# Turning attention weights: TensorE transposes against VectorE 32x32 blocks and quadrant DMAs

## The chip, the core and the metric

The kernel is one program on one core of a Trainium2 chip. The metric is the device time of one execution in microseconds (us), the median of several runs. The engines are TensorE (PE in the profile; PEld is its weight load), VectorE (DVE), ScalarE (ACT), GpSimd (POOL) and SyncE (SP), which here only issues DMAs.

## The reference, cut to what matters

Four graph layers follow each other on x of 32 batches x 256 nodes x 128 features; after each one the input is added and the rows are normalised. All is float32. The third layer (attention) and the fourth (two graph convolutions and four LSTM sweeps) are where the change lies:

```
# layer 3: attention over the 256 nodes
Wh = h @ W;  s1 = Wh @ a1;  s2 = Wh @ a2
e = s1[:, :, None] + s2[:, None, :];  e = where(e >= 0, e, 0.2 * e)
e = where(adj == 0, -inf, e);  h' = softmax(e, axis=-1) @ Wh
# layer 4
h = relu(adj @ (x @ Wg0 + bg0));  h = relu(adj @ (h @ Wg1 + bg1))
for p in 1..4:  h[p-1::p] = last hidden state of an LSTM over windows of p nodes
```

## The kernel before

The 32 batches are worked in 8 groups of 4 (GB = 4). The first two layers need sums over all batches and come first; groups 0 and 1 of layer 3 are worked on their own; then a loop of slots (`slots`, s = 2 to 10) runs three things side by side, written out by hand in each engine's program: attention of group s (A, s = 2 to 7), graph convolution of group s - 1 (B), LSTM of group s - 2 (L), and the last normalisation of group s - 3 (T). Each engine works its own list strictly in order, and semaphores tie the lists together.

The LSTM has eleven steps a group, k = 0 to 10. For step k TensorE works `x(k)` (line 855: input part) and `h(k)` (line 867: recurrent part, which needs the hidden state of step k - 1), ScalarE the gates' tanh (line 1231), VectorE `inner(k)` (lines 1712, 1718, 1722), ScalarE the cell's tanh (line 1267), and VectorE `state(k)` (line 1740), which releases `h(k + 1)`.

Attention of a group: ScalarE writes the exponentials of batch b into E1 (`a_exps`, line 1194, two instructions of 256 columns and their accumulator reads); E1 has the target node on the partitions and the source node along the columns. The mixing matmul (`a_mix`, line 791: two matmuls of 256 columns a batch, two records each) contracts over source nodes, so E1 must be turned. Before, TensorE does that: `a_turn_e` (line 770) works 16 transposes of 128x128 a group into PSUM, after `x(8)` and ahead of `h(8)`, and VectorE copies them into MS (`a_weights`, line 1640, four copies of 512 columns). Then come `h(8)`, `x(9)`, `a_mix` for batches 0 to 2, `a_project_mix` (line 801) for 0 and 1, `h(9)`, `x(10)`, `a_mix` for batch 3, and the rest. `a_hidden` (line 1700) is the relu of the second graph convolution on VectorE: it reads all of PSUM tensor PA, into which line 838 has written, and its result is read by `x(0)` of the next slot.

SP's list holds the loads at the start, and then one output DMA a group (line 425), which waits for GpSimd's last normalisation.

MS and E1 are planes 0 and 1 of `late`, a part of the on-chip tensor HB; a plane has 2048 columns, and COLS is 1024, so a half plane (h = 0 or 1) holds two batches.

Of the kernel before, what the change touches and what calls it, by code (L numbers as in the profile page):

```python
# [27 lines left out]
GB = 4  # L28
# [72 lines left out]
def build(nc, x, xt, adj, early_in, later_in, lstm_w, out):  # L101
    ctx = ExitStack()
    with ctx:
# [18 lines left out]
        MS, E1 = (late[:, k, :].rearrange("p (t n) -> p t n", n=NODES) for k in range(2))  # L122
        HS = late[:, 3, 0:2 * BANK].rearrange("p (k n) -> p k n", k=2)
        ZF = late[:, 3, 2 * BANK:4 * BANK]

        AN = late[:, 0, 0:BANK].rearrange("p (c n) -> p c n", c=NC)
        DIAG = late[:, 2, 0:NC * P].rearrange("p (c n) -> p c n", c=NC)
# [105 lines left out]
        def before(g):  # L233
# [15 lines left out]
        agg0_ps, loop_ok, first_ok, second_ok, both_ok, mix1, mix3, norm_ok, diag_ok, turned_ok = (  # L249
            sem(n) for n in ("agg0_ps", "loop_ok", "first_ok", "second_ok", "both_ok", "mix1", "mix3", "norm_ok", "diag_ok",  # L250
                             "turned_ok"))
        copied_ok = sem("copied_ok")
        f_half, cf_half, cell_half, tc_half = (sem(n) for n in ("f_half", "cf_half", "cell_half", "tc_half"))
        lane1 = [sem(f"{n}_lane1") for n in ("g_ps", "g_ok", "ca_ok", "cf_ok", "cell_ok", "tc_ok", "h_ok")]
        rows_ok, dots_ok, s12_ok, px_ps, px_ok = (sem(n) for n in ("rows_ok", "dots_ok", "s12_ok", "px_ps", "px_ok"))
# [140 lines left out]
        @block.sync  # L396
        def _(sp):
            def load_xt(g):
                sp.dma_start(XT[:, g % NX], xt[g]).then_inc(xt_in[g % NX], 16)

            def load_x(g):
                sp.dma_start(XIN[:, g % NX], x[g]).then_inc(x_in[g % NX], 16)

            sp.dma_start(AD[:, 1], adj[:, 1]).then_inc(adjt_in, 16)
            load_x(0)
            sp.dma_start(early[:], early_in).then_inc(early_ok, 16)
            load_xt(0)
            sp.dma_start(AD[:, 0], adj[:, 0]).then_inc(adj_in, 16)
            load_x(1)
            load_xt(1)  # L410
            load_x(2)
            load_xt(2)
            sp.dma_start(later[:], later_in).then_inc(later_ok, 16)
            load_xt(3)
            load_x(3)
            for g in range(NX, GROUPS):
                sp.wait_ge(gate_ps, g - NX + 1) if g - NX < DIRECT else sp.wait_ge(gate_x, g - NX + 1 - DIRECT)
                load_xt(g)
                sp.wait_ge(mix3, g - NX + 1)
                load_x(g)  # L420
            sp.dma_start(WT[:], lstm_w).then_inc(lstm_in, 16)

            for g in range(GROUPS - 1):
                sp.wait_ge(ln[3]["out"], TILES * (g + 1))
                sp.dma_start(out[g], OUT[:, g % 2]).then_inc(sent[g % 2], 16)
            half = TILES // 2 * P
            sp.wait_ge(last_act, TILES // 2)
            sp.dma_start(out[GROUPS - 1][:, 0:half], OUT[:, 1, 0:half]).then_inc(sent[1], 16)
            sp.wait_ge(last_dve, LAST_DVE)
            sp.wait_ge(last_act, TILES - LAST_DVE)  # L430
            sp.dma_start(out[GROUPS - 1][:, half:], OUT[:, 1, half:]).then_inc(sent[1], 16)
            sp.wait_ge(sent[0], 16 * (GROUPS // 2))
            sp.wait_ge(sent[1], 16 * (GROUPS // 2 + 1))
# [129 lines left out]
        def _(pe):  # L563
# [221 lines left out]
            def a_mix(g, some):  # L785
                pe.wait_ge(ln[1]["out"], TILES * (g + 1))
                f = front(g)
                for b in some:
                    pe.wait_ge(pt_ok, GB * (g - 1) + b + 1)
                    for m in range(NC):  # L790
                        mm = pe.matmul(f.AB[b][:, 0:NODES], turned(X2, m, b), f.MS[:, 2 * b + m, :],  # L791
                                       start=(m == 0), stop=(m == NC - 1))
                    mm.then_inc(px_ps, 1)

# [124 lines left out]
            def slot(s, par, A, B, L, T):  # L919
                def x(k):  # L920
                    lstm_x(s - 2, par, k) if L else None

                def h(k):
                    lstm_h(s - 2, k) if L else None

                if s == LAST + 2:
                    lstm_x(LAST, par, 0)
                    t_turn(s - 3, 1 - par)
                    lstm_x(LAST, par, 1)
                    for k in range(LANED, NSTEP):  # L930
                        for l in range(2):

                            if STEPS[k][1] == 0:
                                lane_x(par, k, l)
                                lane_x(par, k + 1, l) if k > LANED and l == 0 else None
                            else:
                                lane_x(par, k, l) if STEPS[k][1] > 1 or l == 1 or k == LANED + 1 else None
                                lane_h(k, l)
                    t_turn_half(par, 0)
                    spin(Q[F][:, 0:P], 8)  # L940
                    t_turn_half(par, 1)
                    return
                if not L and not A and not B:
                    return

                if s == LAST + 1:
                    x(0)
                    x(1)
                    t_turn(s - 3, 1 - par)
                    a_spread0(LAST, (0, 1), 0)  # L950
                    x(2)
                    x(3)
                    h(3)
                    a_spread0(LAST, (2, 3), 1)
                    a_weigh0(LAST, 0)
                    spin(PB[:, BANK:BANK + P], 4)
                    x(4)
                    a_weigh0(LAST, 1)
                    x(5)
                    h(5)  # L960
                    x(6)
                    a_weigh1(LAST)
                    h(6)
                    a_spread1(LAST)
                    for k in range(7, NSTEP):
                        x(k)
                        h(k) if STEPS[k][1] else None
                    return
                x(0)
                a_residual(s) if A else None  # L970
                x(1)
                t_turn(s - 3, 1 - par) if T else None
                a_spread0(s - 1, (0, 1)) if B else None
                x(2)
                a_spread0(s - 1, (2, 3)) if B else None
                x(3)
                h(3)
                a_rows(s) if A else None
                a_weigh0(s - 1) if B else None
                x(4)  # L980
                x(5)
                h(5)
                x(6)
                a_weigh1(s - 1) if B else None
                h(6)
                a_spread1(s - 1) if B else None
                x(7)
                x(8)
                a_turn_e(s, range(GB)) if A else None
                h(8)  # L990
                x(9)
                if A:
                    a_mix(s, (0, 1, 2))
                    a_project_mix(s, (0, 1))
                h(9)
                x(10)
                if A:
                    a_mix(s, (3,))
                    a_project_mix(s, (2,))
                h(10)  # L1000
                a_project_mix(s, (3,)) if A else None
# [57 lines left out]
        def _(act):  # L1059
# [115 lines left out]
            def a_lin(g, some):  # L1175
                f = front(g)
                for b in some:
                    act.wait_ge(wh_ok, 2 * g + b // 2 + 1) if g < 2 else act.wait_ge(s12_ok, g - 1)
                    act.wait_ge(max_ok, TILES * g + 2 * b + 2)
                    reach(act, et_ps, GB * before(g))  # L1180
                    for c in range(NC):
                        t = 2 * b + c
                        s1 = f.WH[:, t, P:P + 1] if g < 2 else S12[:, 0, t:t + 1]
                        e = act.activation(f.E1[:, t], f.MS[:, t], ACT.Prelu, bias=s1, scale=1.0, alpha=SLOPE)
                    e.then_inc(lin_ok, 1)
# [83 lines left out]
            def slot(s, par, A, B, L, T):  # L1269
# [38 lines left out]
                state(6)  # L1308
                a_exps(s, (1, 2)) if A else None
                gates(7)  # L1310
                a_exps(s, (3,)) if A else None
                state(7)
                cell(8)
                a_mixed(s, (0, 1, 2)) if A else None
                cell(9)
# [56 lines left out]
        def _(dve):  # L1372
# [249 lines left out]
            def a_bias(g, h=None):  # L1622
# [10 lines left out]
                dve.scalar_tensor_tensor(out=f.EB[:, ts], in0=f.ZM[:, ts], scalar=SLOPE, in1=f.ZM[:, ts], op0=ALU.mult,  # L1633
                                         op1=ALU.min).then_inc(eb_ok, size(h))

            def a_weights(g, some):
                f = front(g)
                for b in some:
                    dve.wait_ge(et_ps, GB * g + b + 1)
                    dve.tensor_copy(f.MS[:, 2 * b:2 * b + 2].rearrange("p m n -> p (m n)"), f.AB[b]).then_inc(pt_ok, 1)  # L1640
# [189 lines left out]
            def slot(s, par, A, B, L, T):  # L1830
# [45 lines left out]
                cell(5)  # L1876
                t_stats(s - 3) if T else None
                a_biased1(s - 1) if B else None
                cell(6)
                a_hidden(s - 1, 1 - par) if B else None  # L1880
                norm_small(3, 2, s - 3) if T and A else None
                cell(7)
                norm_small(3, 2, s - 3) if T and not A else None
                a_weights(s, (0, 1)) if A else None
                cell(8)
                if A:
                    a_weights(s, (2, 3))
                    a_inverse(s)
                    a_sum2_mix(s, (0, 1))
                cell(9)  # L1890
# [95 lines left out]
```

## Time and profile before

| | before |
|---|---|
| median of 3 runs (lowest, highest) | 634.5 us (633.63, 634.8) |
| the profiled execution | 635.21 us |
| its span, first to last instruction | 633.4 us |
| mean granted TensorE clock | 0.996 |
| TensorE busy | 617.9 us (98%) |
| VectorE busy | 470.4 us (74%) |
| ScalarE busy | 435.6 us (69%) |
| GpSimd busy | 167.3 us (26%) |

The span is what the trace shows; 1.8 us of the profiled time lie around it. Each engine's busy time is a union of its instructions. Matmuls are pipelined: a group's printed duration reaches over the start of the next one, so the pace of TensorE is read from the distance between starts. A wait for several semaphores is put down to the one that came last.

### The profile page before, as it was taken

Reading aid. Unit: us, or ns where it says so; the run is one execution under the profiler, and the core shown is the slowest. Engines: PE = TensorE matmul, PEld = TensorE weight load, DVE = VectorE, ACT = ScalarE, POOL = GpSimd, SP = SyncE. Lnnn points to the kernel's source line nnn. Section 1 sums busy time; section 2 is a strip of 40 time slices with the busy share of each in tenths; the row PEclk is TensorE's granted clock in tenths of the full one; section 3 lists DMA queues with packets and bytes.
Section 4 is the critical chain, followed back from the end, with each engine's and each line's share of the span. In section 5 each row is a group of like instructions: output and inputs, shape, how many; then the busy total and the mean of one; then the engine's idle time right before and its main releaser. Section 6 shows DMA issues by size and latency. Waiting matters only on the chain.

```text
span 633.4 us, 9530 instructions
## 1 busy us (share of the span) xinstructions
PE 617.9 (98%) x2738; PEld 433.9 (68%) x2738; DVE 470.4 (74%) x1623; ACT 435.6 (69%) x1000; POOL 167.3 (26%) x228
## 2 busy tenths in 40 slices
PE   9999999999999999999999999999999999999994
PEld 6645556448975686578568757865885686577794
DVE  3999999877847658866887787688769867365656
ACT  3678786957847765784777678567857766546774
POOL 1465541005332003204403240340143032103201
PEclk9999999999999999999999999999999999999998
DMA  8334000000000000000000000000000000000000
GB/s 331 136 130 167 1 2 0 0 1 2 1 1 1 1 2 0 2 1 34 2 1 1 33 2 1 35 2 1 1 33 2 0 35 1 1 0 35 1 35 35
DMA packets 4372, 16.85 MB, mean 27 GB/s; under 512 B 480, under 2 KB 480, under 8 KB 4192
## 3 DMA queue, kind: packets, MB, share of 16 engines
q1 hardware_dynamic: 4320, 16.25, 6.7%
q8 instruction: 22, 0.36, 0.2%
q14 instruction: 30, 0.25, 0.1%
HBM read 12.05 MB, written 4.19 MB: 26 GB/s over the span
## 4 chain that ended last, share of the span: by engine, by line
PE 77%; DVE 3%; ACT 3%; issue 2%; POOL 1%; ACTq 0%; POOLq 0%; DVEq 0%
PE QQ L855 26%; PE QQ L867 15%; PE PA L838 4%; PE PA L810 4%; PE PB L829 2%; PE PB L820 2%; PE PB L691 2%; PE PA L691 2%; PE PA L791 2%; PE PB L791 2%; PE PA L644 1%; PE QQ L889 1%; PE PB L908 1%; PE PB L770 1%; PE PA L770 1%
## 5 line engine op out<-in xcount | busy, mean ns | idle before, releaser
L1231 ACT ACTIVATE raw<-QQ,BL 128x256 f32<-128x256 f32 (+2 forms) x279 | 150.1, 558 | 75.1 <-PE QQ L867 37.7
L855 PE MATMUL QQ<-HT,WT 128*128 128x256 f32 (+2 forms) x558 | 183.9, 474 | 1.1 <-ACT raw L1231 0.6
L450 POOL TENSOR_TENSOR RSD<-VAR,pw 128x4 f32<-128x4 f32 (+1 forms) x43 | 61.8, 1438 | 376.2 <-DVE VAR L1454 376.2
L855 PEld LDWEIGHTS QQ<-HT,WT 128*128 128x128 f32 x558 | 103.5, 190 | 59.3 <-issue 28.3
L867 PE MATMUL QQ<-HB,WT 128*128 128x256 f32 (+2 forms) x336 | 100.2, 441 | 0.4 <-DVE HB L1740 0.2
L867 PEld LDWEIGHTS QQ<-HB,WT 128*128 128x128 f32 x336 | 61.2, 190 | 29.3 <-issue 13.4
L1267 ACT ACTIVATE raw<-raw 128x256 f32<-128x256 f32 (+4 forms) x79 | 37.1, 470 | 25.9 <-DVE raw L1722 19.7
L1712 DVE SCALAR_TENSOR_TENSOR raw<-raw 128x256 f32<-128x256 f32 (+2 forms) x60 | 32.5, 542 | 20.2 <-ACT raw L1231 19.6
L1740 DVE SCALAR_TENSOR_TENSOR HB<-raw 128x256 f32<-128x256 f32 (+4 forms) x42 | 20.1, 478 | 23.5 <-ACT raw L1267 23.5
L1066 ACT ACTIVATE X<-Z,OFF,RSD 128x128 f32<-128x128 f32 x80 | 31.8, 481 | 2.5 <-POOL OFF L456 2.5
L518 POOL TENSOR_SCALAR X<-four,MEAN,RSD 128x128 f32<-128x128 f32 x64 | 30.7, 494 | 1.6
L1194 ACT ACTIVATE HB<-HB,EB 128x256 f32<-128x256 f32 x64 | 30.9, 501 | 0.2
L644 PE MATMUL PA<-AHT,X 128*128 128x256 f32 x128 | 29.6, 384 | 1.3 <-ACT X L1066 1.3
L810 PE MATMUL PA<-AD,X 128*128 128x256 f32 x128 | 30.3, 379 | 0.0
L531 POOL TENSOR_SCALAR four<-HB,MEAN,RSD 128x128 f32<-128x128 f32 x56 | 29.6, 543 | 0.7
L658 PE MATMUL QQ<-one_b,later 128*128 128x512 f32 x64 | 29.1, 597 | 0.6 <-ACT one_b L1100 0.6
L838 PE MATMUL PA<-AD,Y 128*128 128x256 f32 x128 | 29.2, 380 | 0.0
L644 PEld LDWEIGHTS PA<-AHT,X 128*128 128x128 f32 x128 | 23.7, 190 | 7.7 <-issue 4.8
L810 PEld LDWEIGHTS PA<-AD,X 128*128 128x128 f32 x128 | 23.8, 191 | 6.8 <-issue 4.1
L838 PEld LDWEIGHTS PA<-AD,Y 128*128 128x128 f32 x128 | 24.2, 190 | 4.3
L621 PE MATMUL PB<-four,AD 128*128 128x512 f32 x56 | 26.2, 611 | 0.0
L1112 ACT ACTIVATE HB<-QQ 128x512 f32<-128x512 f32 x32 | 18.0, 587 | 11.5 <-PE QQ L658 10.1
(254 smaller groups left out, 1164.5 us busy)
## 6 DMA issues: line engine op xcount, KB each, us to landing
four<-in_x SPq DMA_DIRECT2D x8, 512.0 KB, 4.0
raw<-in_xt SPq DMA_DIRECT2D x8, 512.0 KB, 6.6
out<-four SPq DMA_DIRECT2D x7, 512.0 KB, 2.7
WT<-in_lstm SPq DMA_DIRECT2D x1, 2048.0 KB, 9.3
later<-in_later SPq DMA_DIRECT2D x1, 725.5 KB, 10.2
AD<-in_adj SPq DMA_DIRECT2D x2, 256.0 KB, 4.8
out<-four SPq DMA_DIRECT2D x2, 256.0 KB, 2.0
early<-in_early SPq DMA_DIRECT2D x1, 289.0 KB, 4.7
```

The lines of the kernel that those rows point to most:

```text
L450: pool.tensor_tensor(RSD[kk][:, ts], VAR[kk][:, ts], pw[:, ts], ALU.pow).then_inc(ln[k]["rstd"], some)
L518: pool.tensor_scalar(tile_of(X1, g, c, b), nth(f.Z2, t), MEAN[f.kk2][:, t:t + 1], RSD[f.kk2][:, t:t + 1], ALU.add, ALU.mult).then_inc(ln[2 ...
L644: mm = pe.matmul(PA[:, b * NODES:(b + 1) * NODES], tile_of(X1, g, m, b), AHT[:, m, :], start=(m == 0), stop=(m == NC - 1))
L810: mm = pe.matmul(PA[:, b * NODES:(b + 1) * NODES], tile_of(X1, g, m, b), ADJT[:, m, :], start=(m == 0), stop=(m == NC - 1))
L838: mm = pe.matmul(PA[:, b * NODES:(b + 1) * NODES], turned(Y, m, b), ADJT[:, m, :], start=(m == 0), stop=(m == NC - 1))
L855: mm = pe.matmul(steps_view(Q[q], k), WT[:, 0, (p - 1) * 4 + q, :], ht_view(par, k), start=True, stop=(s == 0))
L867: pe.matmul(Q[q][:, 0:nw * GB], WT[:, 1, (p - 1) * 4 + q, :], HS[:, (k - 1) % 2, 0:nw * GB], start=False, stop=True).then_inc(g_ps, 1)
L1066: act.activation(nth(to, t), nth(z, t), ACT.Identity, bias=OFF[kk][:, t:t + 1], scale=RSD[kk][:, t:t + 1]).then_inc(ln[k]["out"], 1)
L1194: e = act.activation(f.E1[:, t], f.E1[:, t], ACT.Exp, bias=f.EB[:, t:t + 1], scale=1.0, accum_out=DEN[:, t:t + 1] if g > 1 else None)
L1231: act.activation(TG[q][:, at:n], Q[q][:, at:n], ACT.Tanh, scale=0.5 if q == G else 0.25, bias=BL[:, p - 1, q:q + 1]).then_inc(g_ok, 1)
L1267: act.activation(TC[:, at:n], CELL[:, at:n], ACT.Tanh, scale=0.5).then_inc(tc_ok, 1)
L1712: dve.scalar_tensor_tensor(out=target[:, 0:n], in0=TG[I][:, 0:n], scalar=1.0, in1=TG[G][:, 0:n], op0=ALU.add, op1=ALU.mult).then_inc(cell_ ...
```

## The change

It touches the slots s = 2 to 7 alone; groups 0 and 1 keep TensorE's transposes. In those six slots:

- `a_turn_e` leaves TensorE's list (16 transposes) and `a_weights` VectorE's (four copies).
- VectorE gets `a_turn_blocks`: one block transpose a batch, 128 partitions x 512 columns, of each 32x32 block of E1 in its place, written to MS in an order that puts together what goes to one partition quadrant. Batch 0 comes after `inner(6)`, 1 and 2 after `state(6)`, 3 after `state(7)`.
- SP gets `move_blocks`: for each half, a wait for the two block transposes of its batches, then 16 DMAs, one for each pair of a source and a target quadrant (32 partitions x 256 columns, 32 KB), from MS into E1. The slot's output DMA stands behind the 32 DMAs.
- `a_mix` waits for all 16 DMAs of its half in place of VectorE's copy, and reads E1 with a rearranged column order. It also waits for the reader of the PSUM bank that it writes (`y1_ok`, `h1_ok`).
- `a_hidden` moves from behind `state(6)` to behind the last block transpose.
- On ScalarE the last `a_exps` moves behind the tanh of cell 7; `a_lin` waits from group 3 on for the mixing matmuls instead of the transposes.

```diff
--- before.py
+++ after.py
@@ -122,6 +122,10 @@
         MS, E1 = (late[:, k, :].rearrange("p (t n) -> p t n", n=NODES) for k in range(2))
         HS = late[:, 3, 0:2 * BANK].rearrange("p (k n) -> p k n", k=2)
         ZF = late[:, 3, 2 * BANK:4 * BANK]
+
+        def by_block(k, h):
+
+            return late[:, k, h * COLS:(h + 1) * COLS].rearrange("p (q b c m i) -> p q b c m i", q=4, b=2, c=NC, m=NC)
 
         AN = late[:, 0, 0:BANK].rearrange("p (c n) -> p c n", c=NC)
         DIAG = late[:, 2, 0:NC * P].rearrange("p (c n) -> p c n", c=NC)
@@ -249,7 +253,8 @@
         agg0_ps, loop_ok, first_ok, second_ok, both_ok, mix1, mix3, norm_ok, diag_ok, turned_ok = (
             sem(n) for n in ("agg0_ps", "loop_ok", "first_ok", "second_ok", "both_ok", "mix1", "mix3", "norm_ok", "diag_ok",
                              "turned_ok"))
-        copied_ok = sem("copied_ok")
+        copied_ok, tr_ok = sem("copied_ok"), sem("tr_ok")
+        moved_ok = [sem(f"moved_ok{k}") for k in range(2)]
         f_half, cf_half, cell_half, tc_half = (sem(n) for n in ("f_half", "cf_half", "cell_half", "tc_half"))
         lane1 = [sem(f"{n}_lane1") for n in ("g_ps", "g_ok", "ca_ok", "cf_ok", "cell_ok", "tc_ok", "h_ok")]
         rows_ok, dots_ok, s12_ok, px_ps, px_ok = (sem(n) for n in ("rows_ok", "dots_ok", "s12_ok", "px_ps", "px_ok"))
@@ -420,9 +425,22 @@
                 load_x(g)
             sp.dma_start(WT[:], lstm_w).then_inc(lstm_in, 16)
 
-            for g in range(GROUPS - 1):
-                sp.wait_ge(ln[3]["out"], TILES * (g + 1))
-                sp.dma_start(out[g], OUT[:, g % 2]).then_inc(sent[g % 2], 16)
+            def move_blocks(g, h):
+
+                sp.wait_ge(tr_ok, GB * (g - 2) + 2 * (h + 1))
+                for q in range(4):
+                    for c in range(4):
+                        sp.dma_start(late[32 * c:32 * c + 32, 1, h * COLS + q * NODES:h * COLS + (q + 1) * NODES],
+                                     late[32 * q:32 * q + 32, 0, h * COLS + c * NODES:h * COLS + (c + 1) * NODES]).then_inc(moved_ok[h], 16)
+
+            for s in range(2, GROUPS + 2):
+                if s < GROUPS:
+                    for h in range(2):
+                        move_blocks(s, h)
+                if s >= 3:
+                    g = s - 3
+                    sp.wait_ge(ln[3]["out"], TILES * (g + 1))
+                    sp.dma_start(out[g], OUT[:, g % 2]).then_inc(sent[g % 2], 16)
             half = TILES // 2 * P
             sp.wait_ge(last_act, TILES // 2)
             sp.dma_start(out[GROUPS - 1][:, 0:half], OUT[:, 1, 0:half]).then_inc(sent[1], 16)
@@ -786,9 +804,11 @@
                 pe.wait_ge(ln[1]["out"], TILES * (g + 1))
                 f = front(g)
                 for b in some:
-                    pe.wait_ge(pt_ok, GB * (g - 1) + b + 1)
+                    pe.wait_ge(moved_ok[b // 2], 256 * (g - 1))
+                    reach(pe, h1_ok if b % 2 else y1_ok, 2 * g)
                     for m in range(NC):
-                        mm = pe.matmul(f.AB[b][:, 0:NODES], turned(X2, m, b), f.MS[:, 2 * b + m, :],
+                        mm = pe.matmul(f.AB[b][:, 0:NODES].rearrange("p (c q i) -> p c q i", c=NC, q=4), turned(X2, m, b),
+                                       by_block(1, b // 2)[:, :, b % 2, :, m, :].rearrange("p q c i -> p c q i"),
                                        start=(m == 0), stop=(m == NC - 1))
                     mm.then_inc(px_ps, 1)
 
@@ -986,7 +1006,6 @@
                 a_spread1(s - 1) if B else None
                 x(7)
                 x(8)
-                a_turn_e(s, range(GB)) if A else None
                 h(8)
                 x(9)
                 if A:
@@ -1177,7 +1196,7 @@
                 for b in some:
                     act.wait_ge(wh_ok, 2 * g + b // 2 + 1) if g < 2 else act.wait_ge(s12_ok, g - 1)
                     act.wait_ge(max_ok, TILES * g + 2 * b + 2)
-                    reach(act, et_ps, GB * before(g))
+                    reach(act, et_ps, GB * before(g)) if g <= 2 else act.wait_ge(px_ps, GB * (g - 2))
                     for c in range(NC):
                         t = 2 * b + c
                         s1 = f.WH[:, t, P:P + 1] if g < 2 else S12[:, 0, t:t + 1]
@@ -1308,8 +1327,8 @@
                 state(6)
                 a_exps(s, (1, 2)) if A else None
                 gates(7)
+                state(7)
                 a_exps(s, (3,)) if A else None
-                state(7)
                 cell(8)
                 a_mixed(s, (0, 1, 2)) if A else None
                 cell(9)
@@ -1633,6 +1652,14 @@
                 dve.scalar_tensor_tensor(out=f.EB[:, ts], in0=f.ZM[:, ts], scalar=SLOPE, in1=f.ZM[:, ts], op0=ALU.mult,
                                          op1=ALU.min).then_inc(eb_ok, size(h))
 
+            def a_turn_blocks(g, some):
+
+                for b in some:
+                    dve.wait_ge(exps_ok, GB * g + b + 1)
+                    dve.wait_ge(lin_ok, GB * g + 2 * (b // 2 + 1))
+                    dve.transpose(by_block(0, b // 2)[:, :, b % 2].rearrange("p q c m i -> p (c m) q i"),
+                                  E1[:, 2 * b:2 * b + 2].rearrange("p c (m q i) -> p (c m) q i", m=NC, q=4)).then_inc(tr_ok, 1)
+
             def a_weights(g, some):
                 f = front(g)
                 for b in some:
@@ -1876,15 +1903,19 @@
                 cell(5)
                 t_stats(s - 3) if T else None
                 a_biased1(s - 1) if B else None
-                cell(6)
-                a_hidden(s - 1, 1 - par) if B else None
+                inner(6)
+                a_turn_blocks(s, (0,)) if A else None
+                state(6)
+                a_hidden(s - 1, 1 - par) if B and not A else None
                 norm_small(3, 2, s - 3) if T and A else None
+                a_turn_blocks(s, (1, 2)) if A else None
                 cell(7)
                 norm_small(3, 2, s - 3) if T and not A else None
-                a_weights(s, (0, 1)) if A else None
+                if A:
+                    a_turn_blocks(s, (3,))
+                    a_hidden(s - 1, 1 - par)
                 cell(8)
                 if A:
-                    a_weights(s, (2, 3))
                     a_inverse(s)
                     a_sum2_mix(s, (0, 1))
                 cell(9)
```

## Rows read from the trace of the kernel before

**Rows 1.** The page: span, busy time by engine, chain that ended last by engine.

```profile
span 633.4 us, 9530 instructions
...
PE 617.9 (98%) x2738; PEld 433.9 (68%) x2738; DVE 470.4 (74%) x1623; ACT 435.6 (69%) x1000; POOL 167.3 (26%) x228
...
PE 77%; DVE 3%; ACT 3%; issue 2%; POOL 1%; ACTq 0%; POOLq 0%; DVEq 0%
```

**Rows 2.** Timeline, TensorE: start us, us, engine, line, operation, output<-input, count.

```profile
341.67 0.60 PE L770 MATMUL PB<-ident,HB 128*128 128x128 f32 x4
...
343.41 1.89 PE L867 MATMUL QQ<-HB,WT 128*128 128x256 f32 x8
...
346.87 1.03 PE L791 MATMUL PB<-HB,X 128*128 128x256 f32 x4
...
348.59 1.03 PE L791 MATMUL PB<-HB,X 128*128 128x256 f32 x4
```

**Rows 3.** Same timeline, VectorE and ScalarE in the same stretch.

```profile
337.21 0.51 DVE L1740 SCALAR_TENSOR_TENSOR HT<-raw 128x340 f32<-128x340 f32 x1 [0.68 <-ACT raw L1267]
...
337.50 0.50 ACT L1194 ACTIVATE HB<-HB,EB 128x256 f32<-128x256 f32 x1
...
338.90 2.02 DVE L1700 TENSOR_SCALAR HT<-PA 128x1024 f32<-128x1024 f32 x1 [1.18 <-PE PA L838]
339.28 1.34 ACT L1231 ACTIVATE raw<-QQ,BL 128x256 f32<-128x256 f32 x3 [0.20 <-PE QQ L855]
...
340.76 0.17 DVE L1444 TENSOR_TENSOR SUM<-STL 128x16 f32<-128x16 f32 x1
...
341.00 0.50 ACT L1194 ACTIVATE HB<-HB,EB 128x256 f32<-128x256 f32 x1
...
341.50 0.42 DVE L1712 SCALAR_TENSOR_TENSOR raw<-raw 128x256 f32<-128x256 f32 x1
...
342.48 0.43 DVE L1740 SCALAR_TENSOR_TENSOR HB<-raw 128x256 f32<-128x256 f32 x1 [0.55 <-ACT raw L1267]
...
342.82 0.68 DVE L1640 COPY HB<-PB 128x512 f32<-128x512 f32 x1
```

**Rows 4.** One line, L791, over the whole span: count, first and last start.

```profile
L791 PE MATMUL PA<-HB,X x48: 379/379/379, 232.7 to 527.0; 128*128 128x256 f32 x48
```

**Rows 5.** Timeline of SP's queue, its DMA issues: start us, us of issuing.

```profile
2.09 0.43 SPq L399 DMA_DIRECT2D raw<-in_xt  x1
2.56 0.43 SPq L408 DMA_DIRECT2D AD<-in_adj  x1
...
6.31 0.43 SPq L402 DMA_DIRECT2D four<-in_x  x1
...
20.82 0.33 SPq L402 DMA_DIRECT2D four<-in_x  x1
21.20 0.44 SPq L399 DMA_DIRECT2D raw<-in_xt  x1
```

**Rows 6.** The page, DMA issues: count, KB each, median us to landing.

```profile
out<-four SPq DMA_DIRECT2D x7, 512.0 KB, 2.7
...
out<-four SPq DMA_DIRECT2D x2, 256.0 KB, 2.0
```

**Rows 7.** Half-microsecond stretches at the end: us, PE busy (records), PEclk, DMA.

```profile
625.50:626.00 0.50, 0.44 (x4) 1.00 0.00 0
...
628.50:629.00 0.50, 0.00 (x0) 0.50 0.00 0
```

**Rows 8.** Timeline, TensorE, at the start of the span.

```profile
1.03 4.64 PE L567 MATMUL QQ<-ones 128*128 128x128 f32 x20 [1.03 <-DVE ones L1399]
5.52 4.52 PE L621 MATMUL PB<-four,AD 128*128 128x512 f32 x8
...
13.40 3.59 PE L621 MATMUL QQ<-four,AD 128*128 128x512 f32 x8
```

## The prediction

> **What bounds the kernel now.** I read the page first. TensorE is busy 98% of the span, VectorE 74%, and the chain that ended last lies on TensorE for 77% of the span [rows 1]. Then the timeline of one slot's end, on all engines. On TensorE one group starts where the one before it leaves off, with no wait: the 16 transposes take 341.67 to 343.41, h(8) starts at 343.41, the mixing of batch 0 at 346.87 and of batch 2 at 348.59 [rows 2]. The other engines' waits beside it are waits for TensorE's results, so time taken from TensorE's list in a slot is gained, and a hole put into it is lost. The timeline of SP says what its DMAs cost: nearly nothing is on that queue in the slots, and the only bursts are the loads at the start [rows 5].
>
> **What is taken away.** 16 transposes from 341.67 to 343.41 are 1.74 us, 0.109 us each. The change is made in six slots; the mixing matmuls of the line stand from 232.7 to 527.0, in these six slots alone [rows 4]. So at most 6 x 1.74 = 10.4 us can be gained, if nothing new is waited for.
>
> **What covered the hidden state of step 7.** The transposes stood between x(8) and h(8). Before, VectorE's state(7) starts at 342.48 and ends near 342.9, because a_hidden holds VectorE from 338.90 to 340.76 and the six small normalisation steps until inner(7) at 341.50 [rows 3]. Left so, h(8) could start at 342.9 and 1.2 of the 1.74 us would be lost. The change moves both: a_hidden goes behind the last block transpose, the small steps go ahead of gate 7. The gates' tanh starts at 339.28 and takes 1.34 us for three, so the second, which inner(7) needs, is done near 340.2; from inner(7) to state(7) it is 0.98 us (341.50 to 342.48) and state(7) takes 0.43 [rows 3]: released near 341.6, while TensorE is through with x(8) at 341.67. The cover just holds, and I cost this at nothing.
>
> **VectorE.** Four copies of 512 columns go, 0.68 us each [rows 3]; four block transposes of 512 columns come. No row shows a block transpose. The bounds are the 256-column operation (0.42) and half of the 1024-column one that also writes in a turned order (2.02, so 1.0) [rows 3]; I take 0.68, the copy of as many columns. a_hidden now ends at about 342.8 + 2.0 = 344.8, before the mixing of batch 1 wants its bank (346.0), and holds inner(8) back by about 1.5 us; h(9) stands behind three mixings and two projections, so this is covered. On ScalarE the last exponentials (before: until about 341.5, the last starting at 341.00 [rows 3]) end near 342.1 behind the tanh of cell 7, so the last block transpose ends at about 342.8.
>
> **SP: the term that decides.** Each slot adds 32 DMA issues to a queue that had one output issue, and the last of each 16 must land before its mixing may start. An issue takes SP 0.43 us in the burst of loads, with 0.47 from start to start (2.09 to 2.56); a pair in mid-run has 0.33 and then 0.44, 0.38 apart (20.82 and 21.20); the nine from 2.09 to 6.31 are 0.53 apart on average [rows 5]. These move 256 KB to 725 KB each, and the issuing time shows no trend with the bytes. But all of them have 128 partitions and the new ones 32: a price per row is not excluded by any row. I take 0.47, as an instruction of the same kind with the queue full behind it; the ends are 0.33 with no gap and 0.53, and below them a quarter of 0.33, which is a rival below.
>
> From issue to landing: 2.7 us for 512 KB and 2.0 for 256 KB [rows 6]. The straight line through both gives 1.4 us for 32 KB, an estimate from these two rows; 2.0 is the upper end.
>
> The start: state(6) on VectorE starts at 337.21 and ends by 337.7; the small steps take 0.74 (340.76 to 341.50), so the block transpose of batch 1 starts at about 338.45 (its exponentials, started at 337.50, are done by then [rows 3]) and ends at about 339.15. SP starts at 339.2.
> - First half: 339.2 + 15 x 0.47 + 1.4 = 347.65. TensorE gets to batch 0 at 346.87 - 1.74 = 345.13 and waits 2.5 us.
> - Second half: its block transposes are done at 342.8, but SP is still issuing the first half, so its 32nd issue starts at 339.2 + 31 x 0.47 = 353.8 and lands at 355.2. TensorE has worked batches 0 and 1 by 347.65 + 1.72 = 349.4 and waits 5.8 us for batch 2.
>
> Before, batch 2 started at 348.59 [rows 2]; now at 355.2: 6.6 us later in each slot, the 1.74 us already in it. TensorE has no idle time after that in which to catch up, since nothing else kept it waiting. The output DMA of the slot comes behind the 32 issues, some 7 us later than now; nobody waits for it within the slot. Data is not the limit: 32 KB per 0.47 us is far less than 512 KB in 2.7 us.
>
> The Trainium skill, "VectorE: DVE Perf Modes", section "Rules for kernel authors", speaks against the change: it gives a 128x128 transpose to TensorE where PSUM will do as its target. In this trace such a transpose costs TensorE 0.109 us, and two issues on SP cost 0.94. The skill's "DMA: Bandwidth & Descriptors", "Anatomy of one DMA", gives about 50 ns for the sequencer's dispatch of a DMA (on GpSimd's path); by it the first rival holds and the time is 624.8. No issue in this trace is under 0.33 us.
>
> **The clock.** TensorE's granted clock was 1.00 until its last matmul at 625.9 and 0.50 at 628.5, 2.5 us later [rows 7]; that is 1.2 in place of 2.4 GHz. A hole of 5.8 us is more than twice as long, so I expect the clock to fall in it. Its price: at the start, where TensorE came from standing still, 20 matmul records of 128 columns took 4.64 us, against 20 x 0.109 = 2.2, and the first eight of line 621 took 4.52 against 3.59 later [rows 8], together 3.4 us. Bounds 0 and 3.4 a slot; I take 1.6, near the middle, since no row shows a fall in mid-run.
>
> **Sum.** 6 x (6.6 + 1.6) = 49 us on 635.2 (span 633.4 and 1.8 around it; the median of the runs is 634.5, 0.1% away): 684.
>
> **Rivals.**
> - *Issues of 32 partitions are cheap* (faster). Where the price goes with the partitions, an issue is a quarter, 0.08 us, and with the gap 0.12. The second half then starts at 342.8 and lands at 342.8 + 15 x 0.12 + 1.4 = 346.0, before TensorE gets to batch 2 at 346.85: no wait, and the whole 10.4 us is gained: 624.8. It decides below 0.18 us an issue; at 0.26 (339.2 + 31 x 0.26 + 1.4 = 348.6) gain and loss are equal. For it: the rows have 128 partitions only. Against it: none lies below 0.33, whatever it moves. 0.12.
> - *Cheap issues, but h(8) waits* because the cover of step 7 fails (a block transpose of over 1 us, or the exponentials late): about 1.2 us of the 1.74 lost in each slot, 635.2 - 6 x 0.5 = 632. 0.02.
> - *Issues near break-even*, 0.25 to 0.27: 634 to 637, no measurable change. 0.03.
> - *The forecast's mechanism, at its lower end*: 0.33 an issue and no loss of clock. 339.2 + 31 x 0.33 + 1.4 = 350.8, 2.2 later a slot: 648. At 0.38: 352.4, 3.8 later: 658 without and 668 with 1.6 for the clock.
> - *At its upper end*: 0.53, landing 2.0, block transposes at 1.0 (two of them ahead of SP's start, 0.7 more) and 3.4 for the clock: 357.6 + 0.7 - 348.6 = 9.7, and 6 x 13.1 = 79: 714.
> - That the change doesn't do what it says I don't see: line 770 leaves the six slots by the diff.
>
> **How the numbers follow.** SP's issues bound the mixing, whatever their price between 0.28 and 0.53: 0.83. Within it the time is likeliest near 684. Outside stand the cheap issues, 0.14 together, and the break-even, 0.03. The range 646 to 714 holds about 0.8. About 0.2%, 1.3 us, can be told from no change: faster 0.14, same 0.03, slower 0.83.
>
> **What would show it.** In the timeline of SP after: 32 issues a slot back to back, 0.4 to 0.5 us apart, from some 2.4 us before x(8) ends to 12 us behind that. In the waits: TensorE's mixing (its line or its weight load) waiting for DMA, twice a slot, about 2.5 and 6 us, 50 us in all; TensorE's busy share well under 98%; the granted clock at 0.50 for a part of each slot. VectorE's block transposes near 0.7 us, no wait of h(8) for state(7). Wrong it would be if SP's issues were 0.1 us apart and the mixing waited for nothing; a little wrong if the second wait were 3 us (issues at 0.35 to 0.4) or if the clock stayed at 1.00.

## The result, and the profile after

The changed kernel takes 721.6 us (median; 720.35 to 722.04) against 634.4 for the kernel before, a ratio of 1.137 with a 95% interval of 1.135 to 1.139: 87 us slower. The sign and the mechanism were forecast, the size was not: 684 us, with 646 to 714 as the range.

From the page of the changed kernel (against [rows 1] and [rows 6]): span, busy time, granted clock by slice, the chain that ended last, the new DMAs with their median time from issue to landing.

```profile
span 719.5 us, 9542 instructions
...
PE 632.6 (88%) x2642; PEld 438.2 (61%) x2642; DVE 470.8 (65%) x1623; ACT 435.7 (61%) x1000; POOL 166.8 (23%) x228
...
PEclk9999999999999599959997999699969996999998
...
PE 59%; SPq 16%; DVE 5%; issue 3%; ACT 3%; DMA 2%; POOL 1%; POOLq 0%; DVEq 0%; ACTq 0%
...
HB<-HB SPq DMA_DIRECT2D x192, 32.0 KB, 1.8
```

TensorE worked 632.6 us, 15 more than before although the transposes are gone, of a span 86 us longer; 16% of the chain that ended last now lies on SP's queue, which was not in it. PEclk is the granted clock in tenths, for 40 slices of the span: 9 (90% or more) in every slice but the last before, now between 5 and 7 in six single slices, one for each slot of the change.

One slot's end on the timeline (this stretch answers to [rows 2] and [rows 3]; columns are start, length, engine, line, operation, count, idle time and releaser). Line 1660 is the block transpose, 433 SP's issues, 1767 `state(k)`, 887 `h(k)`, 875 `x(k)`, 810 the mixing.

```profile
368.35 1.41 DVE L1660 STREAM_TRANSPOSE HB<-HB 128x512 f32<-128x512 f32 x2
...
369.09 20.14 SPq L433 DMA_DIRECT2D HB<-HB  x32
...
371.13 0.47 DVE L1767 SCALAR_TENSOR_TENSOR HB<-raw 128x256 f32<-128x256 f32 x1 [0.55 <-ACT raw L1286]
...
371.66 1.99 PE L887 MATMUL QQ<-HB,WT 128*128 128x256 f32 x8
...
373.49 1.89 PE L875 MATMUL QQ<-HT,WT 128*128 128x256 f32 x8
...
380.44 1.80 PE L810 MATMUL PB<-HB,X 128*128 128x256 f32 x4 [5.06 <-issue]
...
382.04 1.91 PE L810 MATMUL PA<-HB,X 128*128 128x256 f32 x4
...
390.52 2.07 PE L810 MATMUL PB<-HB,X 128*128 128x256 f32 x4 [6.57 <-DMA HB<-HB]
...
395.95 1.89 PE L875 MATMUL QQ<-HT,WT 128*128 128x256 f32 x8
```

VectorE and ScalarE do what was forecast: the block transposes of batches 1 and 2 take 1.41 us together, `state(7)` ends at 371.60, and h(8) starts at 371.66, where x(8) leaves off. SP starts at 369.09 and needs 20.14 us for 32 issues, 0.63 from start to start. TensorE ends x(9) near 375.4, waits until 380.44, mixes batches 0 and 1, and waits again until 390.52 for batch 2. Over all six slots:

```profile
PE PB L810 <- DMA HB<-HB: 41.1, 6, 7.9
PE PB L810 <- issue: 30.4, 6, 5.2
```

The wait put down to "issue" is the one for the first half: the 16th issue starts near 378.5 and the mixing 1.9 us later, as it does behind the 32nd. Together they are 71.5 us, where some 50 were forecast.

### The profile page after: what moved, and what is told of

It is laid out like the page before. It is cut to its first block, busy times and chain, and to the rows that moved or that the text cites. A ratio compares the mean times of both kernels' runs of the same rounds, so it can differ in the third digit from the quotient of the medians.

```text
span 719.5 us, 9542 instructions
## 1 busy us (share of the span) xinstructions
PE 632.6 (88%) x2642; PEld 438.2 (61%) x2642; DVE 470.8 (65%) x1623; ACT 435.7 (61%) x1000; POOL 166.8 (23%) x228
## 4 chain that ended last, share of the span: by engine, by line
PE 59%; SPq 16%; DVE 5%; issue 3%; ACT 3%; DMA 2%; POOL 1%; POOLq 0%; DVEq 0%; ACTq 0%
PE QQ L875 19%; SPq L433 16%; PE QQ L887 11%; PE PA L830 4%; PE PB L849 2%; PE PB L840 2%; PE PB L709 2%; PE PB L810 2%; PE PA L709 2%; DMA HB<-HB 2%; DVE HB L1660 1%; PE PB L821 1%; PE PA L821 1%; PE QQ L909 1%; PE PA L662 1%
## 5 line engine op out<-in xcount | busy, mean ns | idle before, releaser
L887 PE MATMUL QQ<-HB,WT 128*128 128x256 f32 (+2 forms) x336 | 102.5, 449 | 0.4 <-DVE HB L1767 0.2
L810 PE MATMUL PB<-HB,X 128*128 128x256 f32 x48 | 24.5, 665 | 71.5 <-DMA HB<-HB 41.1
L887 PEld LDWEIGHTS QQ<-HB,WT 128*128 128x128 f32 x336 | 63.0, 196 | 31.5 <-issue 13.4
L1691 DVE SCALAR_TENSOR_TENSOR four<-PB,RD,X 128x128 f32<-128x128 f32 x24 | 7.3, 346 | 102.6 <-PE PB L821 102.6
L810 PEld LDWEIGHTS PB<-HB,X 128*128 128x128 f32 x48 | 13.9, 318 | 80.2 <-DMA HB<-HB 45.4
L1191 ACT ACTIVATE one_a<-PB 128x256 f32<-128x256 f32 x12 | 4.6, 384 | 88.7 <-PE PB L810 88.7
L536 POOL TENSOR_SCALAR X<-four,MEAN,RSD 128x128 f32<-128x128 f32 x64 | 32.4, 522 | 1.6
```

The lines of the kernel that those rows point to most:

```text
L536: pool.tensor_scalar(tile_of(X1, g, c, b), nth(f.Z2, t), MEAN[f.kk2][:, t:t + 1], RSD[f.kk2][:, t:t + 1], ALU.add, ALU.mult).then_inc(ln[2 ...
L810: mm = pe.matmul(f.AB[b][:, 0:NODES].rearrange("p (c q i) -> p c q i", c=NC, q=4), turned(X2, m, b), by_block(1, b // 2)[:, :, b % 2, :, m ...
L887: pe.matmul(Q[q][:, 0:nw * GB], WT[:, 1, (p - 1) * 4 + q, :], HS[:, (k - 1) % 2, 0:nw * GB], start=False, stop=True).then_inc(g_ps, 1)
```

## The experiments

### Without the quadrant DMAs

```diff
-                        move_blocks(s, h)
...
-                    pe.wait_ge(moved_ok[b // 2], 256 * (g - 1))
+                    pe.wait_ge(tr_ok, GB * (g - 2) + b + 1)
-                                       by_block(1, b // 2)[:, :, b % 2, :, m, :]
+                                       by_block(0, b // 2)[:, :, b % 2, :, m, :]
```

> The quadrant DMAs are left out (the output lacks the exchange between quadrants); the mixing reads the block transposes where VectorE wrote them. Theory, SP's issues carry the whole loss: nothing is waited for, the 16 transposes are gained in full, 635.2 - 10.4 = 625 us, granted clock near 1.00. Rival, a part of the loss comes from VectorE's and ScalarE's new order or from the mixing's rearranged operand: over 634 us, with h(8) or the mixing waiting for VectorE.

Measured: 624.59 us, a ratio of 0.985 (0.983 to 0.987) to the kernel before. Its timeline at the same place, h(8) and the mixing of batches 0 and 2:

```profile
338.49 1.99 PE L884 MATMUL QQ<-HB,WT 128*128 128x256 f32 x8
...
342.05 1.03 PE L807 MATMUL PB<-HB,X 128*128 128x256 f32 x4
...
343.78 1.03 PE L807 MATMUL PB<-HB,X 128*128 128x256 f32 x4
```

From h(8) to batch 0 it is 3.56 us, to batch 2 5.29; before it was 3.46 and 5.18 [rows 2]. So little else in the change costs anything: the block transposes, the new order on VectorE and ScalarE and the rearranged operand of the mixing are hidden, and 9.2 of the forecast 10.4 us are gained. All the loss, some 97 us against this kernel, is in the exchange between quadrants.

### The cover of step 7

```diff
 e1_no_move, VectorE:
                 state(6)
-                a_hidden(s - 1, 1 - par) if B and not A else None
+                a_hidden(s - 1, 1 - par) if B else None
                 norm_small(3, 2, s - 3) if T and A else None
-                a_turn_blocks(s, (1, 2)) if A else None
                 cell(7)
...
-                    a_turn_blocks(s, (3,))
-                    a_hidden(s - 1, 1 - par)
+                    a_turn_blocks(s, (1, 2, 3))
```

> e1_no_move with a_hidden and the six small steps put back ahead of gate 7 on VectorE, as in the kernel before, and the block transposes 1 to 3 behind state(7). Theory, the transposes covered the hidden state of step 7: h(8) waits from 341.67 to 342.9, 1.2 us a slot, 624.6 + 6 x 1.2 = 632 us. Rival, there is slack elsewhere: 625.

Measured: 631.87 us, 7.3 more than without this edit. h(8) now stands idle for VectorE's hidden state (idle time and releaser in brackets):

```profile
341.20 1.99 PE L884 MATMUL QQ<-HB,WT 128*128 128x256 f32 x8 [1.12 <-DVE HB L1764]
```

1.12 us in this slot: the transposes did cover the late hidden state, and without the move of `a_hidden` most of what they free would have gone there.

### What an issue costs

Each slot issues its 32 DMAs in another form, given here in short; the source line is the same. The kernel was run once.

```diff
+ g == 2: sp.wait_ge(moved_ok[h], 16 * (4 * q + c))   # ahead of each but the first
+ g == 3: late[:, 1, j:j + 64] <- late[:, 0, j:j + 64]
+ g == 4: late[rows, 1, block] <- x[0][32 * q:32 * q + 32, c * NODES:(c + 1) * NODES]
+ g == 5: late[:, 1, j:j + 64] <- x[0][:, j - h * COLS:j - h * COLS + 64]
+ g == 6: 32 partitions x 32 columns, late <- late
+ g == 7: 8 partitions x 256 columns, late <- late
```

> A price list: each of the six slots issues its 32 DMAs in another form (the output lacks the exchange between quadrants in all but the first): slot 2 as changed, but each DMA waits for the landing of the one before; 3: 128 partitions x 64 columns, on chip; 4: 32 partitions x 256 columns from HBM; 5: 128 x 64 from HBM; 6: 32 x 32, on chip (4 KB); 7: 8 partitions x 256, on chip (8 KB). Theory A, a fixed price an instruction, more with both ends on chip: about 0.59 in slots 3, 6 and 7, 0.43 in 4 and 5, and 0.5 in slot 2, where none stands before it. Theory B, the price goes with rows: 0.59 in 6, about 0.15 in 7, four times 0.59 in 3. Theory C, it goes with bytes or with the transfers in flight: 6 and 7 below 0.4, slot 2 at 0.33.

The line's issues slot by slot, 2 (its last ten) to 7; shortest, median and longest in ns, first and last start in us:

```profile
L453 SPq DMA_DIRECT2D HB<-HB x10: 507/507/507, 262.8 to 278.8; - x10
...
L453 SPq DMA_DIRECT2D HB<-HB x32: 465/601/1326, 331.4 to 352.2; - x32
...
L453 SPq DMA_DIRECT2D HB<-in_x x32: 345/421/431, 404.0 to 418.3; - x32
...
L453 SPq DMA_DIRECT2D HB<-in_x x32: 347/432/866, 471.0 to 486.1; - x32
...
L453 SPq DMA_DIRECT2D HB<-HB x32: 565/591/601, 537.4 to 557.0; - x32
...
L453 SPq DMA_DIRECT2D HB<-HB x32: 624/625/736, 608.7 to 629.8; - x32
```

- One at a time (first row): 507 ns. In a row, 128 partitions x 64 columns (second): 601. 32 x 32, an eighth of the bytes (fifth): 591. 8 partitions (last): 625.
- With the source in HBM (rows three and four): 421 and 432, for 32 and 128 partitions.

So theory A: a price an instruction, on chip nearly the same for 8 and 128 partitions and for 4 and 32 KB, and higher by 0.17 where both ends are on chip. What stands ahead adds to it as well; the output DMA of the slot, 0.33 us alone, behind either kind:

```profile
418.74 0.42 SPq L462 DMA_DIRECT2D out<-four  x1
...
557.64 0.58 SPq L462 DMA_DIRECT2D out<-four  x1
```

0.42 behind loads from HBM, 0.58 behind the on-chip copies. The first rival of the prediction, a price by the partition, falls. In one slot the landing of each was waited for before the next: there the issues lie 1.78 apart (16.0 us over nine), that is 0.51 for the issue and 1.27 until the landing is seen.

### Four wide DMAs, and eight narrow ones, a half

```diff
 four:
-                    for c in range(4):
-                        sp.dma_start(late[32 * c:32 * c + 32, 1, ...], late[32 * q:32 * q + 32, 0, ...])
+                    sp.dma_start(late[:, 1, cols], late[:, 0, cols])
 eight:
-                    for c in range(4):
+                    for c in range(2):
```

> The same bytes a half, in 4 DMAs of 128 partitions x 256 columns in place of 16 of 32 partitions (straight copies, so the output lacks the exchange between quadrants). Theory, the number of issues is the price: at 0.63 us each the second half is issued from 342.8 on in the clock of the slot before and lands at 342.8 + 3 x 0.63 + 2.0 = 346.7, just before the mixing of batch 2 wants it (346.85): 625 to 628 us. Rival, the bytes or the rows are the price: SP's issues take four times as long and the time stays near 720.

Measured: 627.24 us, 0.989 (0.988 to 0.991) of the kernel before, with the same bytes as the full exchange, as straight copies. The number of issues was the price; the bytes are not.

> Eight of the 16 DMAs a half (two of four target quadrants; the other blocks stay unturned in the output). Theory, 0.63 us an issue: second half lands at 339.2 + 15 x 0.63 + 1.8 = 350.5, 1.9 us later than the mixing of batch 2 before; 635.2 + 6 x 1.9 = 646 us, up to 6 more where the clock falls in the hole of 3.3 us. Rival, a fixed price of the exchange (landing, or the first issue) outweighs the number: over 680.

Measured: 656.71 us, above the forecast 646 to 652. Its timeline (columns as above):

```profile
348.57 10.02 SPq L433 DMA_DIRECT2D HB<-HB  x16
...
359.88 1.13 PE L810 MATMUL PB<-HB,X 128*128 128x256 f32 x4 [3.05 <-DMA HB<-HB]
...
365.13 1.89 PE L875 MATMUL QQ<-HT,WT 128*128 128x256 f32 x8
...
482.39 1.13 PE L810 MATMUL PB<-HB,X 128*128 128x256 f32 x4 [3.05 <-DMA HB<-HB]
...
485.98 1.89 PE L875 MATMUL QQ<-HT,WT 128*128 128x256 f32 x8
```

The granted clock behind these two waits (columns: stretch, length, PE busy and records, granted clock, DMA share, GB/s):

```profile
362.00:363.00 1.00, 1.00 (x4) 0.50 0.00 0
...
484.00:485.00 1.00, 1.00 (x8) 1.00 0.00 0
```

The last of 16 issues starts near 358.0 and the mixing of batch 2 at 359.88: 1.9 us. The hole before it, expected at 3.3 us, is 3.05 here and 3.3 on the mean of the six slots. What was undersized is the clock. From the mixing of batch 2 to x(10) it is 5.25 us in this slot, with a granted clock of 0.50 in between. Two slots later it is 3.59 at a clock of 1.00, behind a hole of the same 3.05 us. Over the six slots the clock cost 1.7 us in four, 3.0 in the first and nothing in that one, 9.6 in all.

### The clock kept up

```diff
+                    reach(pe, h1_ok if b % 2 else y1_ok, 2 * g)
+                    spin(f.AB[b][:, 0:P], {0: 22, 2: 36}.get(b, 0))
                     pe.wait_ge(moved_ok[b // 2], 256 * (g - 1))
-                    reach(pe, h1_ok if b % 2 else y1_ok, 2 * g)
```

> The changed kernel with idle matmuls on TensorE put ahead of its two waits for DMA (22 and 36 of 128 columns, 4.8 and 7.9 us). Theory, the clock costs what the rows after the second landing show (mixing 1.87 for 0.86, projections 1.70 for 0.89, h(9) 0.13 more: 1.95 us a slot): 721.6 - 6 x 1.95 = 710 us, granted clock near 1.00. Rival, the time behind the landing is set by something else than the clock: 720 to 722 at a granted clock of 1.00.

Measured: 713.27 us at a mean granted clock of 0.998, 8.3 less than the changed kernel, 11.7 forecast. SP's issues, the mixing of batch 2 and x(10):

```profile
365.39 20.93 SPq L433 DMA_DIRECT2D HB<-HB  x32
...
387.63 1.13 PE L811 MATMUL PB<-HB,X 128*128 128x256 f32 x4 [0.90 <-DMA HB<-HB]
...
391.22 1.89 PE L876 MATMUL QQ<-HT,WT 128*128 128x256 f32 x8
```

From the mixing of batch 2 to x(10) it is 3.59 us, 5.43 in the changed kernel: 1.84 in this slot for the clock, where 1.95 was expected. What is missing lies on SP: its 32 issues take 20.93 us here and 20.14 there, since single issues take 1.3 to 1.8 us in five of the six slots, where it was two of six in the changed kernel; from the first issue to the last it is 3.2 us more over the six slots. Why some issues take two to three times the usual wasn't settled.

### Half of it: two batches by blocks, two by TensorE

```diff
                 x(8)
+                a_turn_e(s, (0, 1)) if A else None
                 h(8)
                 x(9)
...
-                    a_mix(s, (0, 1, 2))
+                    a_mix(s, (0, 1))
                     a_project_mix(s, (0, 1))
                 h(9)
                 x(10)
...
-                    a_mix(s, (3,))
+                    a_mix(s, (2, 3))
```

(and on SP only the second half's 16 DMAs, on ScalarE the exponentials of batches 2 and 3 first, on VectorE `a_hidden` ahead of gate 7)

> Half of the change: batches 2 and 3 of a group are turned by blocks and 16 DMAs, and mixed behind x(10); batches 0 and 1 stay with TensorE's transposes. ScalarE works the exponentials of 2 and 3 first. Theory: SP starts at 338.7 in the clock of the slot before, the last of 16 lands at 338.7 + 15 x 0.63 + 1.8 = 350.0, and the mixing of batch 2 wants it at 352.1: no wait, eight transposes a slot gained, 6 x 0.87 = 5.2: 629 us. Rival, h(8) waits for step 7 or the later mixing delays the slot's tail: 634 or more.

Measured: 632.06 us, 0.996 (0.994 to 0.997): 2.6 of the forecast 5.2 us.

```profile
337.49 10.56 SPq L437 DMA_DIRECT2D HB<-HB  x16
...
346.40 0.61 PE L831 MATMUL PB<-later,one_a 128*128 128x128 f32 x4
...
347.04 0.71 PE L831 MATMUL PA<-later,one_a 128*128 128x128 f32 x4
...
351.04 1.03 PE L820 MATMUL PB<-HB,X 128*128 128x256 f32 x4
```

The DMAs are hidden: issued from 337.49, the last lands ahead of the mixing at 351.04. The time lies between the forecast 629 and the rival's 634. Of the missing 2.6 us small waits show 1.7: the projection of batch 1 starts 0.64 behind that of batch 0, where 0.44 is its pace, because ScalarE's copy stands directly ahead of it now; and h(8) waits half a microsecond for the hidden state of step 7 in one slot. The rest stays open.

### The exchange by way of HBM

```diff
-                for q in range(4):
-                    for c in range(4):
-                        sp.dma_start(...)
+                reach(sp, moved_ok[h], 64 * (g - 2))
+                sp.dma_start(turn[h], late[:, 0, h * COLS:(h + 1) * COLS]).then_inc(put_ok[h], 16)
+                sp.wait_ge(put_ok[h], 16 * (g - 1))
+                for c in range(4):
+                    sp.dma_start(late[32 * c:32 * c + 32, 1, h * COLS:(h + 1) * COLS].rearrange("p (q n) -> p q n", q=4),
+                                 turn[h].rearrange("(q i) (c n) -> c i q n", q=4, c=4)[c]).then_inc(moved_ok[h], 16)
```

(batches 2 and 3 are mixed behind x(10), as in the experiment above, and on VectorE the block transpose of batch 1 stands ahead of the six small steps)

> The whole exchange between quadrants by way of HBM: a half is written with one DMA of 128 partitions and read back with four of 32 partitions x 4 x 256 columns, 5 issues in place of 16, and batches 2 and 3 are mixed behind x(10). Theory, the number of issues is what counts: first half 338.8 + 2.3 for the write + 4 issues of 0.45 + 2.0 = 344.9, just before the mixing of batch 0 (345.1); second half about 349 against 351: no wait or a short one, 625 to 629 us. Rival, two landings in a row cost more than the issues they save (over 3 us each): the mixing of batch 0 waits over 1.7 us a slot, and the time is over 635.

Measured: 630.25 us, 0.993 (0.992 to 0.995) of the kernel before, a little over the forecast 625 to 629. SP's first half, and TensorE's mixing of batch 0 and the first two projections:

```profile
337.24 0.34 SPq L434 DMA_DIRECT2D turn<-HB  x1
...
339.92 1.74 SPq L437 DMA_DIRECT2D HB<-turn  x4
...
344.21 1.10 PE L814 MATMUL PB<-HB,X 128*128 128x256 f32 x4 [0.44 <-issue]
...
346.01 0.61 PE L825 MATMUL PB<-later,one_a 128*128 128x128 f32 x4
...
346.65 0.71 PE L825 MATMUL PA<-later,one_a 128*128 128x128 f32 x4
```

In HBM a read can take its rows from all four quadrants, so five issues do the work of 16; the four reads take 1.74 us together. Two landings stand in a row, 2.7 us for the write (337.24 to 339.92) and about 3.0 from the last read's issue to the mixing of batch 0 (344.21), which so still waits 0.6 us behind x(9); the second projection, as above, 0.2.

```diff
 ScalarE:
-                    a_exps(s, (0,))
-                    a_lin(s, (2,))
+                    a_exps(s, (0, 1))
                 gates(6)
-                a_lin(s, (3,)) if A else None
+                a_lin(s, (2,)) if A else None
                 state(6)
-                a_exps(s, (1, 2)) if A else None
+                a_lin(s, (3,)) if A else None
+                a_exps(s, (2,)) if A else None
 VectorE: both block transposes of the first half right behind inner(6)
 TensorE:
-                    a_project_mix(s, (0, 1))
+                    a_project_mix(s, (0,))
                 h(9)
+                a_project_mix(s, (1,)) if A else None
```

> e7_dram with its two remaining waits taken away: ScalarE works the exponentials of batch 1 ahead of gate 6 (two linear parts move behind it) and VectorE both block transposes of the first half right behind inner(6), so SP starts at about 338 in the clock of the slot before, 1 us earlier; and the projection of batch 1 stands behind h(9). Theory: the waits of 0.6 us at the mixing of batch 0 and 0.2 at the projection of batch 1 go, 630.25 - 6 x 0.8 = 625.5 us. Rival, the hidden state of step 6 comes later and x(7) waits: 630 or more.

Measured: 624.57 us, 0.985 (0.984 to 0.987) of the kernel before: as fast as the kernel with no exchange at all (624.59), with the whole computation done.

```profile
333.34 0.34 SPq L434 DMA_DIRECT2D turn<-HB  x1
...
336.01 1.74 SPq L437 DMA_DIRECT2D HB<-turn  x4
...
339.07 1.89 PE L879 MATMUL QQ<-HT,WT 128*128 128x256 f32 x8
...
340.80 1.03 PE L814 MATMUL PB<-HB,X 128*128 128x256 f32 x4
```

SP starts 3.9 us ahead of h(8) (337.24), in place of 2.8; the first half has landed when x(9) (339.07, 1.73 long) leaves off at 340.80, and the mixing starts there. This is the version to keep.

## Why the prediction was right, and where it fell short

- **TensorE is the bound, and a hole in its list is lost: right.** The time grew by what it waited and by what the clock took from it.
- **The transposes are worth 10.4 us: nearly.** 9.2 and 9.6 us in the two kernels that have all of the gain; 10.0 in the span of the first.
- **The cover of step 7 holds, worth 1.2 us a slot: right.** h(8) starts where x(8) leaves off; with the cover taken away it waits 1.12 us in the slot shown, and 7.3 us are lost in all.
- **VectorE: right.** 0.71 us a block transpose, 0.68 taken.
- **The start of SP: right.** 2.5 us ahead of h(8) forecast, 2.57 measured.
- **The price of an issue: wrong, and this is the step that failed.** 0.47 us was taken from the burst of loads [rows 5], which have their source in HBM; the new DMAs have both ends on chip and cost 0.63. The rows couldn't show that, since none of them is an on-chip copy; the text doubted the number of partitions, which doesn't matter, and not the two ends, which do. Over 31 issues it is 31 x 0.16 = 5.0 us a slot, 30 in all. The upper end, 0.53, was an average of the same kind of DMA, so the range was drawn too low with it.

```profile
L433 SPq DMA_DIRECT2D HB<-HB x192: 507/591/1821, 223.1 to 603.4; - x192
```

- **The landing: 1.4 taken, about 1.9 measured** from the last issue's start (388.6) to the mixing (390.52); 0.5 a slot, 3 in all. That is inside the upper end of 2.0; the line through two DMAs to HBM didn't hold for a small one on chip.
- **The clock: right in kind, 1.6 taken, 1.84 measured** in this slot; over the six slots it is 1.5 to 2.5, 2.0 on the mean, 2.3 in all above the forecast. The granted clock by stretches of one microsecond of the same slot (columns: stretch, length, PE busy and records, granted clock, DMA share, GB/s):

```profile
375.00:376.00 1.00, 0.38 (x2) 1.00 0.15 40
380.00:381.00 1.00, 0.56 (x2) 0.85 0.13 34
383.00:384.00 1.00, 0.95 (x3) 0.50 0.21 55
385.00:386.00 1.00, 0.00 (x0) 1.00 0.14 37
388.00:389.00 1.00, 0.00 (x0) 0.50 0.23 62
393.00:394.00 1.00, 1.00 (x7) 0.50 0.00 0
395.00:396.00 1.00, 1.00 (x7) 1.00 0.00 0
```

1.00 as the first hole begins, at 0.50 while batches 0 and 1 are mixed (1.60 us in place of 0.86, hidden by the second wait), back at 1.00 in the second hole, 0.50 again from 388, and up again between 394 and 395, behind the mixing, the projections and the start of h(9). The Trainium skill, "TensorE: Matmul & The Clock Gate", "Part 1: The HAM clock gate", has the two levels, 1.2 and 2.4 GHz; by these rows the trace agrees.

Put together: the second half was to come 6.6 us later than before, and it came 390.52 - 371.66 - 5.18 - 1.74 = 11.9 later; 6 x (11.94 + 1.84) = 83. Two of the six slots have one issue of 1.7 or 1.8 us, some 2.3 more together. Read the same way in every slot, the second half comes 11.9 to 13.5 us later, 74.6 in all, and from the mixing of batch 2 to x(10) it is 1.7 to 2.6 longer than the 3.48 of the kernel before, 12.5 in all: 87.1 of the 87.2 us. Of it 0.1 a slot is h(8), which runs longer, since its first weight load no longer stands ahead of it (371.66 to 373.49, 1.83, against 1.73).

## What to carry to other kernels

Count the DMA instructions that stand between two engines and price each by a row with the same two ends, on chip or HBM: the bytes may be nothing while the issues serialise on one queue. Where one instruction can't express a permutation on chip, a round trip by way of HBM with few, wide DMAs can beat many narrow ones, if its two landings are hidden by starting early. And before engine time is removed, look for what it covered: here a hidden state that would have been 1.1 us late, which only the move of `a_hidden` kept off TensorE.

## What the runs showed of the hardware that was not expected

- SP needs 0.51 us for one on-chip copy and 0.59 to 0.63 in a row (0.63 from start to start for the changed kernel's), with 8 to 128 partitions and 4 to 32 KB, against 0.33 and 0.42 to 0.43 with an end in HBM. The Trainium skill, "DMA: Bandwidth & Descriptors", "Anatomy of one DMA", gives about 50 ns for the sequencer's dispatch on GpSimd's path; SP's issues here are never near that: the shortest, of a read in the exchange by way of HBM, is 0.30 us.
- An issue pays for the one ahead of it: an output DMA of 0.33 us alone takes 0.58 behind on-chip copies.
- With eight DMAs a half, four slots had a hole of 3.05 us on TensorE: in three of them the clock cost 1.7 us behind it, nearly as much as behind one of 6.6 (1.84), and in the fourth nothing.
